# A decoder layer on one core: one output stage, one key decay and one unit's gating issued earlier

## The reference

```python
qkv = silu(x @ qkv_w.T)                    # 32 heads of 128: q, k, v
scores = einsum(q, k) * diag_decay         # causal, decaying with distance
intra = scores @ v
inter = (q * q_decay) @ kv_state           # state of the earlier blocks
kv_state = kv_state * block_decay + (k * k_decay).T @ v
attn = intra + inter
xf = attn * rsqrt(mean(attn * attn) + eps)
out = (sigmoid(x @ gate_w.T) * norm_w * xf) @ out_w.T
```

## Time and profile before

| | before |
|---|---|
| median of 3 runs | 1863.63 us (1861.92 to 1865.05) |
| profiled execution, device time | 1863.91 us |
| its span, first to last instruction | 1862.1 us |
| mean granted TensorE clock | 0.992 |
| TensorE busy | 1775.8 us, 95% |
| VectorE busy | 1329.5 us, 71% |
| ScalarE busy | 970.2 us, 52% |
| GpSimd busy | 641.7 us, 34% |

### The profile page before, as it was taken

How to read it: one execution, slowest core, us unless ns; L and a number is a source line. 1 busy time by engine, 2 the same in 40 slices (tenths; PEclk the granted TensorE clock), 3 DMA queues, 4 the chain that set the end, 5 groups by cost and what they waited for, 6 DMA issues and landing times.

```text
span 1862.1 us, 27416 instructions
## 1 busy us (share of the span) xinstructions
PE 1775.8 (95%) x9865; PEld 893.7 (48%) x9865; DVE 1329.5 (71%) x1867; ACT 970.2 (52%) x1432; POOL 641.7 (34%) x506
## 2 busy tenths in 40 slices
PE   6999999999999999999999999999999999999887
PEld 4454545444454545445454545445454545574333
DVE  7667776767677776767777766667677766659877
ACT  5555454645455454655454444555454444534674
POOL 2352334324342334324333333424333332301433
PEclk9999999999999999999999999999999999999998
DMA  4223224241423224241422214131322214133332
GB/s 172 84 69 108 69 90 108 72 105 46 136 63 108 69 91 108 69 107 46 136 63 69 74 57 108 57 85 46 98 67 68 75 57 108 57 106 122 114 91 91
DMA packets 158116, 161.52 MB, mean 87 GB/s; under 512 B 99872, under 2 KB 127904, under 8 KB 157600
## 3 DMA queue, kind: packets, MB, share of 16 engines
q1 hardware_dynamic: 146528, 147.09, 27.0%
q0 software_dynamic: 2560, 8.39, 1.4%
q10 hardware_dynamic: 8896, 4.28, 0.8%
HBM read 123.56 MB, written 12.58 MB: 73 GB/s over the span
## 4 chain that ended last, share of the span: by engine, by line
PE 67%; DVE 15%; issue 9%; ACT 7%; POOL 1%; DMA 1%; ACTq 0%; DVEq 0%; POOLq 0%
PE bank L1391 16%; PE bank L1393 16%; PE bank L1392 16%; PE bank L1364 4%; PE bank L1478 4%; PE bank L1480 4%; PE bank L1479 4%; DVE w_pair L1743 2%; DVE gated_split L1743 2%; DVE acc L1912 1%; DVE bank L1852 1%; PE bank L1542 1%; PE bank L1553 1%; DVE k_units L1892 1%; ACT L1632 1%
## 5 line engine op out<-in xcount | busy, mean ns | idle before, releaser
L1391 PE MATMUL bank<-x_blocks,w_pair 128*128 128x512 f16 (+1 forms) x1820 | 678.3, 373 | 34.4 <-ACT gate_units L1632 22.9
L1392 PE MATMUL bank<-x_blocks,w_pair 128*128 128x512 f16 (+1 forms) x1820 | 677.9, 372 | 0.0
L1393 PE MATMUL bank<-x_blocks,w_pair 128*128 128x512 f16 (+1 forms) x1820 | 677.9, 372 | 0.0
L1391 PEld LDWEIGHTS bank<-x_blocks,w_pair 128*128 128x128 f16 x1820 | 177.9, 98 | 241.2 <-ACT gate_units L1632 29.8
L2030 POOL TENSOR_TENSOR sums_pair<-raw_pair 128x512 f32<-128x512 f32 x63 | 92.4, 1467 | 563.8 <-DVE w_pair L1743 409.6
L1393 PEld LDWEIGHTS bank<-x_blocks,w_pair 128*128 128x128 f16 x1820 | 178.0, 98 | 202.8
L1392 PEld LDWEIGHTS bank<-x_blocks,w_pair 128*128 128x128 f16 x1820 | 178.1, 98 | 188.6
L1912 DVE TENSOR_TENSOR acc<-acc,bank 128x512 f32<-128x512 f32 x320 | 211.3, 681 | 20.8 <-PE bank L1480 20.5
L1641 ACT ACTIVATE bank<-bank 128x512 f32<-128x512 f32 x145 | 84.7, 584 | 211.1 <-PE bank L1393 210.9
L2056 POOL TENSOR_TENSOR ssq<-ssq,sig 128x512 f32<-128x512 f32 x64 | 81.8, 1278 | 283.8 <-ACT sig L1662 283.8
L1743 DVE SCALAR_TENSOR_TENSOR w_pair<-raw_pair,w_pair 128x1024 f16<-128x1024 f32 x126 | 158.8, 1270 | 21.2 <-ACT w_pair L1606 21.1
(11 more groups left out here) (216 smaller groups left out, 2677.4 us busy)
## 6 DMA issues: line engine op xcount, KB each, us to landing
raw_pair<-w_qk SPq DMA_DIRECT2D x32, 1024.0 KB, 5.5
raw_pair<-w_gate SPq DMA_DIRECT2D x16, 1024.0 KB, 4.9
raw_pair<-w_out SPq DMA_DIRECT2D x16, 1024.0 KB, 4.9
raw_pair<-w_vt SPq DMA_DIRECT2D x15, 1024.0 KB, 5.0
raw_pair<-ctx_in SPq DMA_DIRECT2D x8, 1024.0 KB, 4.9
decay_sb<-rates SPq DMA_DIRECT2D x60, 128.0 KB, 4.5
acc<-x_t SPq DMA_DIRECT2D x4, 1024.0 KB, 11.4
ctx<-raw_pair SPq DMA_DIRECT2D x8, 512.0 KB, 3.0
```

The costliest lines, as they stand in the source:

```text
L1391: pe.matmul(out, w_hi, x_hi, start=unmet and k == 0, stop=False, skip_group_check=halves or not fresh)
L1392: pe.matmul(out, w_hi, x_lo, start=False, stop=False, skip_group_check=halves or not fresh)
L1393: mm = pe.matmul(out, w_lo, x_hi, start=False, stop=k == QT - 1, skip_group_check=halves or not fresh)
```

## The change

Four lists of steps are changed, and nothing is added or left out:

```diff
             "p5": [wo(0)],
-            "p4": sums(S3) + [gate(0)] + split_sum(S3) + [wo(1), attend(2), score(3), gated(2)],
-            "p3": [wo(2), gate(1)] + units(2),
+            "p4": sums(S3) + [gate(0), attend(2), score(3), gated(2)] + split_sum(S3) + [wo(1)],
+            "p3": [gate(1), wo(2)] + units(2),
         })
-        gate_rest = [gate(3), gate(2)]
+        gate_rest = [gate(2), gate(3)]
...
             "p1": [attend(3), gated(3)] + gate_rest,
-            "p2": sums(S2) + [lambda: plan.qk_out("q", 0)] + units(3),
-            "p7": split_sum(S2) + sums(S1) + stages(0) + sums(S4),
+            "p2": sums(S2) + stages(0) + [lambda: plan.qk_out("q", 0)] + units(3),
+            "p7": split_sum(S2) + sums(S1) + sums(S4),
...
             "p5": stages(10) + [part(2)] + [turn(0)],
-            "p4": stages(11),
-            "p3": [part(0), decay(1)],
+            "p4": [decay(1)] + stages(11),
+            "p3": [part(0)],
         })
```

## The result

| | before | after |
|---|---|---|
| median, runs taken side by side (4 each) | 1863.53 us (1861.92 to 1865.05) | 1841.21 us (1839.74 to 1842.91) |
| profiled execution, device time | 1863.91 us | 1839.74 us |
| its span | 1862.1 us | 1837.9 us |
| TensorE busy | 1775.8 us | 1767.7 us |

The ratio is 0.9882, with a 95% interval of 0.9869 to 0.9894: faster by 22.3 us. In the two profiled executions the loop is 21.9 us shorter and the whole span 24.2.

A forecast was written before the change was run, and what follows sets the result against it. TensorE bounds the kernel, so only its standing still can be saved: 13 periods of 1.19 + 0.61 = 1.80 us (23.4), plus 1.4 and 1.24 at the ends, 26.0 us, giving 1837.6 us; range 1823 to 1852 us.

The forecast's parts named there:

- Part 1: attend(2), score(3), gated(2) before S3's split, wo(1); gate(1) before wo(2): attend(3)'s 0.56 us wait goes, VectorE step 0.88 us sooner.
- Part 2: gate(2) before gate(3) on ScalarE: gate(2), which frees the bank for q's product 7, comes 0.53 us sooner.
- Part 3: Output stage 0 before q's product 7: its wait goes, S2's split turns late, 1.19 of 2.57 us a period kept.
- Rival 1: VectorE keeps the port, S2's split does not wait for another GpSimd sum: 39.2 us saved, 1824.4 us; chance 20%.
- Part 4: decay(1) before output stage 11 on VectorE: the 0.61 us wait of v's product 7 goes whole.
- The first group: n=1, TensorE later against other engines, so S2 in time: 0.80 + 0.61 = 1.4 us saved.
- rival 2: ScalarE's wo(2) behind gate(1) keeps attend(3)'s VectorE step late: only 14.6 us saved, 1849.0 us; chance 17%.
- The last group: n=15: attend(3)'s wait for the split of gated(2), 1.24 us, goes.
- The sum: Whole loop: 13 full periods at 1.80 us plus first and last groups, 26.0 us saved.
- 3: Rival: further GpSimd sums ahead of S2's split, 1.27 us a period each: 7 us slower, 1870.6 us; chance 5%.
- 4: Rival: the waits just move to the next place in full, no change; chance 3%.

The follow-up runs named there:

- e2: Kernel before with only attend(2), score(3), gated(2) ahead of S3's split and wo(1), and gate(1) ahead of wo(2); 1857.95 us, ratio 0.995.
- e3: Kernel before with only gate(2) put before gate(3); 1859.85 us, ratio 0.9966.
- e6: Changed kernel with GpSimd's first block sum of the k pair held back until S2 is split; 1819.08 us, ratio 0.9766.
- e1: Kernel before with only decay(1) put ahead of output stage 11; 1858.38 us, ratio 0.9957.
- e7: Changed kernel with wo(2) put back ahead of gate(1); 1835.24 us, ratio 0.9855.
- e5: Changed kernel with unit 3's split moved behind output stage 1, so S2's split comes first; 1817.15 us, ratio 0.9753.
- e9: Control: kernel before the change with GpSimd's first block sum of the k pair held back until S2 is split; 1864.19 us, ratio 0.9999.

## Why the prediction was right, and where it was off

To set the two traces side by side I add 11.13 us to times of after, which puts attend(3) (953.40 there) on the 964.53 of the forecast.

**Part 1, right, its 0.88 too large by 0.12.** attend(3) has no wait. Its first VectorE step stands at 955.39, that is 966.52, against 966.4 forecast. In e2 alone a period gains 0.75 us of the 0.88. The high half of wo(2) starts at 951.59, that is 962.72, and not at 962.6.

**Part 2, right.** 0.53 forecast, 0.52 in e3; product 7 has no wait in the after kernel.

**Part 3, mechanism right, two terms slightly small.** Unit 3's split lost the race by 0.28 us and S2's waited for one more sum, as forecast from an early row of another place; e6 shows that nothing else makes the wait. S2 was ready at 965.90, or 977.03, and 976.89 was forecast; the group began 0.10 after that and not 0.04. So product 5 stands at 966.65, or 977.78, not 977.58: 0.99 us a period were kept and not 1.19. The 0.12 us of Part 1 that the chain came later is most of this. The new wait is there as forecast, but 14 times and not 13, and 1.41 us in the bracket where 1.2 was named. The Trainium skill, page "SBUF — State Buffer", section "Who interferes with whom", which has the two engines exclude each other on the port, is borne out by the durations with and without GpSimd's sum (1.75 us in the after kernel, 0.69 in e6). Rival 1, VectorE keeping the port between two splits queued back to back, was seen at none of the 14 places: S2's split takes 1.75 us at each.

**Part 4, right.** 0.61 us, in e1 and in the whole.

**The first group, wrong.** The forecast had 1.4 us saved at n=1, since TensorE is later there against the other engines and S2 in time. Measured: 0.17 us lost. Product 7's 0.80 and decay(1)'s 0.61 were gained, but S2 was 1.58 late, where nothing was forecast. ScalarE and VectorE of the kernel before at n=1:

```profile
122.57 1.49 ACT L1685 ACTIVATE w_vo<-sums_pair 128x1536 f16<-128x1536 f32 x1
123.94 0.60 ACT L1632 ACTIVATE gate_units<-bank 128x512 f32<-128x512 f32 x1
...
128.07 0.60 ACT L1662 ACTIVATE sig<-bank 128x512 f32<-128x512 f32 x1 [1.28 <-DVE bank L1883]
```

```profile
119.09 1.22 DVE L1743 SCALAR_TENSOR_TENSOR w_vo<-raw_pair,w_vo 128x1024 f16<-128x1024 f32 x1
120.22 0.41 DVE L1879 TENSOR_TENSOR sig<-bank,decay_sb 128x256 f32<-128x256 f32 x1
...
123.38 0.74 DVE L1892 SCALAR_TENSOR_TENSOR k_units<-bank,norm_w_sb,gate_units 128x512 f32<-128x512 f32 x1
124.09 1.76 DVE L1743 SCALAR_TENSOR_TENSOR w_vo<-sums_pair,w_vo 128x1536 f16<-128x1536 f32 x1
```

And of the kernel after:

```profile
123.62 0.60 ACT L1632 ACTIVATE gate_units<-bank 128x512 f32<-128x512 f32 x1
124.10 1.49 ACT L1685 ACTIVATE w_vo<-sums_pair 128x1536 f16<-128x1536 f32 x1
...
128.97 0.60 ACT L1662 ACTIVATE sig<-bank 128x512 f32<-128x512 f32 x1 [2.28 <-DVE bank L1883]
```

```profile
118.95 0.42 DVE L1879 TENSOR_TENSOR sig<-bank,decay_sb 128x256 f32<-128x256 f32 x1 [0.47 <-PE bank L1364]
...
122.97 0.74 DVE L1892 SCALAR_TENSOR_TENSOR k_units<-bank,norm_w_sb,gate_units 128x512 f32<-128x512 f32 x1
...
124.22 1.22 DVE L1743 SCALAR_TENSOR_TENSOR w_vo<-raw_pair,w_vo 128x1024 f16<-128x1024 f32 x1
125.62 1.76 DVE L1743 SCALAR_TENSOR_TENSOR w_vo<-sums_pair,w_vo 128x1536 f16<-128x1536 f32 x1 [0.18 <-ACT w_vo L1685]
```

Before, wo(1) at n=1 was split while attend(2) was still to come, and attend(2) (L1879) found TensorE's result ready. After, attend(2) stands first and waits for TensorE, so gated(2) (L1892) comes only 0.41 us sooner, and the splits of S3 and wo(1) stand behind it. wo(2)'s split comes 1.53 us later and the Square of attend(3) 0.90 later. The advance over TensorE that I counted on is what the reorder gives up, and the wait of 1.58 us stands at n=1 too. In e7 gate(1) is out of the way, wo(2)'s split follows wo(1)'s without a gap, and 0.29 us come back. So rival 2's mechanism, gate(1) ahead of wo(2) on ScalarE, is the smaller part of the loss, and the work now behind gated(2) on VectorE the larger; no run takes that larger part away by itself.

**The last group, right.** 1.24 forecast, 1.25 measured.

**The sum.** 13 x 1.60 - 0.17 + 1.25 = 21.9 us, as in the traces, against 26.0 forecast: 2.6 us are missing by the 0.2 a period and 1.6 by the first group. That the profiled execution, 1839.74 us, comes within 1.8 us of the 1837.9 forecast for it is in part luck: 2.2 us of it were gained behind the loop.

**The rivals.** 1 (1824.4) needed S2 not to wait again, 2 (1849.0) the chain kept everywhere; neither holds, and both give times outside the runs. 3, slower by further sums, didn't occur: no split waited for more than one sum of its own. 4 falls with the three waits that are gone.

## What to carry to other kernels

When a wait is taken away, ask at once how early the next late thing is ready and what it races with. Here 2.57 us were won and 1.58 given back two stages on, at a split that two reorders of a few lines (e5, e6) set free for another 22 to 24 us. The same overlap had cost nothing before (e9): what it costs hangs on the slack around it. A step that is moved behind one that hangs on the bounding engine loses any advance it had, so turns of a loop in which the chains stand differently (the first, the last) need their own sum.

## What was unexpected in the hardware

Where GpSimd's sum and VectorE's split start within 0.02 us of each other, either can come first within one execution (e1 at n=8 and n=9), and in the order of before 1.1 us a period hang on it; in the order of the gate pair after, nothing does (e2 at n=2). Whoever loses waits for the whole of the other: 1.27 us of sum make 1.80 of a 0.68 split, and the reverse makes 1.82 of a 1.27 sum. When VectorE goes straight from one such split to the next while GpSimd has a sum waiting, GpSimd was served first at all 14 places, and never twice in a row there: sum, split, sum, split. A held-up split ends 0.54 to 0.55 us after the sum's end, less than its own 0.69 alone.
